# A transformer layer on one core: projection blocks spread over the steps, and the four score pairs of a step issued together ahead of the contexts

## The reference, cut to what matters

```python
def _L0_attn_ref(hidden_states, Wq, bq, Wk, bk, Wv, bv, Wo, bo):
    q = _split_heads(hidden_states @ Wq + bq)
    k = _split_heads(hidden_states @ Wk + bk)
    v = _split_heads(hidden_states @ Wv + bv)
    scores = jnp.einsum('bhqd,bhkd->bhqk', q, k) * scale
    probs = jax.nn.softmax(scores, axis=-1)
    ctx = jnp.einsum('bhqk,bhkd->bhqd', probs, v)
    return ctx.transpose(0, 2, 1, 3).reshape(b, s, h * d) @ Wo + bo

def _L0_ffn_ref(x, gate_w, up_w, down_w, gate_scale, up_scale, down_scale):
    gate = jax.nn.silu(_quantized_matmul(x, gate_w, gate_scale))
    up = _quantized_matmul(x, up_w, up_scale)
    return _quantized_matmul(gate * up, down_w, down_scale)

x = x + _layernorm(_L0_attn_ref(_layernorm(x), ...))
x = x + _layernorm(_L0_ffn_ref(_layernorm(x), ...))
```

## Time and profile before

| | |
|---|---|
| median of 3 runs | 1830.35 us (1827.28 to 1835.91) |
| the profiled execution's own time | 1833.34 us |
| its span, first to last instruction | 1831.5 us |
| instructions | 23069 |
| mean granted clock of TensorE | 0.941 |
| busy, share of the span | TensorE 89%, VectorE 71%, ScalarE 48%, GpSimd 27% |
| attention pass | until about 1190 us; the rest is the feed-forward pass |

### The profile page before, as it was taken

One profiled execution on the slowest core, in us unless ns is written; L12 is line 12 of the kernel. 1 busy time (PEld: TensorE's weight loads), 2 busy tenths in 40 slices (PEclk: granted clock), 3 DMA queues, 4 the chain that ended last, 5 costly groups with the idle time before them and its releaser, 6 DMA issues.

```text
span 1831.5 us, 23069 instructions
## 1 busy us (share of the span) xinstructions
PE 1621.8 (89%) x8328; PEld 755.8 (41%) x8328; DVE 1304.3 (71%) x2369; ACT 878.4 (48%) x1567; POOL 491.2 (27%) x384
## 2 busy tenths in 40 slices
PE   2599999999999999999999999835699999999996
PEld 1343343343343343343343343123355555555554
DVE  6279879879879879879879878779943543443344
ACT  2236756756756756756756756722222222222222
POOL 4012312212212212212212213345522222222222
PEclk9789999999999999999999999767899999999998
DMA  2402212212212212212112112233010210111020
GB/s 94 97 16 61 68 30 64 60 29 60 64 29 65 59 33 63 57 41 55 57 40 56 58 41 55 70 104 121 23 46 24 70 69 6 64 69 47 24 92 23
DMA packets 76441, 100.91 MB, mean 55 GB/s; under 512 B 15780, under 2 KB 40356, under 8 KB 76324
## 3 DMA queue, kind: packets, MB, share of 16 engines
q1 hardware_dynamic: 76328, 99.44, 18.4%
HBM read 51.65 MB, written 17.83 MB: 38 GB/s over the span
## 4 chain that ended last, share of the span: by engine, by line
PE 72%; DVE 22%; issue 3%; ACT 1%; POOL 1%; DMA 1%; SPq 0%; POOLq 0%; DVEq 0%; ACTq 0%
PE side L924 21%; PE ring L1322 17%; PE contexts L988 11%; PE down_sums L1337 9%; DVE maxima L778 9%; PE scores L976 8%; PE maxima_scores L961 5%; DVE y L737 2%; DVE w_magic L131 2%; DVE qkT L764 1%; DVE denominators L795 1%; DVE denominators L804 1%; DVE ctx_raw L800 1%; DVE xT_low L747 1%; ACT probs L692 1%
## 5 line engine op out<-in xcount | busy, mean ns | idle before, releaser
L778 DVE TENSOR_REDUCE maxima<-maxima_scores 128x1 f32<-128x512 f32 x1024 | 655.8, 678 | 123.7 <-PE maxima_scores L961 119.1
L692 ACT ACTIVATE probs<-scores 128x512 f32<-128x512 f32 x1024 | 554.2, 597 | 362.5 <-PE scores L976 359.5
L961 PE MATMUL maxima_scores<-k_stack,q_stack 64*128 64x512 f16 x1024 | 330.4, 394 | 34.8 <-DVE maxima L778 34.5
L976 PE MATMUL scores<-q_stack,k_stack 64*128 64x512 f16 x1024 | 329.1, 397 | 12.4 <-ACT probs L692 9.3
L988 PE MATMUL contexts<-probs,v_one 128*32 128x512 f32 x2048 | 288.6, 637 | 13.9 <-DVE ctx_raw L800 9.2
L1267 DVE SCALAR_TENSOR_TENSOR fuse<-ring,up_scale,gate 128x512 f32<-128x512 f32 x96 | 71.9, 749 | 263.2 <-PE ring L1322 261.8
L539 POOL TENSOR_TENSOR denominators<-denominators,reciprocals 128x512 f32<-128x512 f32 x33 | 42.4, 1284 | 707.1 <-ACT reciprocals L655 707.1
L1168 POOL TENSOR_TENSOR fuse_low<-fuse,fuse_high 128x512 fp32r<-128x512 f32 x96 | 123.1, 1282 | 368.4 <-ACT fuse_high L1202 368.4
L976 PEld LDWEIGHTS scores<-q_stack,k_stack 64*128 64x128 f16 x1024 | 64.6, 95 | 329.2 <-ACT probs L692 226.2
L1337 PE MATMUL down_sums<-down_q,fuse_high 128*128 128x512 f32 x384 | 171.4, 446 | 30.0 <-POOL fuse_low L1168 30.0
L1337 PE MATMUL down_sums<-down_q,fuse_low 128*128 128x512 f32 x384 | 155.7, 406 | 0.0
(11 more groups left out here) (151 smaller groups left out, 2418.9 us busy)
## 6 DMA issues: line engine op xcount, KB each, us to landing
q_stack<-qkT SPq DMA_DIRECT2D x192, 64.0 KB, 2.0
k_stack<-qkT SPq DMA_DIRECT2D x192, 64.0 KB, 2.0
x_rows<-in_L_attn_hidden_states SPq DMA_DIRECT2D x9, 1024.0 KB, 5.9
x_residual<-in_L_attn_hidden_states SPq DMA_DIRECT2D x36, 256.0 KB, 2.9
middle_rows<-y SPq DMA_DIRECT2D x36, 256.0 KB, 2.9
x_rows_ffn<-middle_rows SPq DMA_DIRECT2D x9, 1024.0 KB, 5.6
x_residual_ffn<-middle_rows SPq DMA_DIRECT2D x8, 1024.0 KB, 7.8
out_rows<-y_ffn SPq DMA_DIRECT2D x32, 256.0 KB, 2.2
```

Of the source, the lines that this page charges most:

```text
L692: act.activation(probs[:, n % 2, j, :], work[(GH * n + j) % RING][:], ACT.Exp, scale=float(D) ** -0.5).then_inc(p_full, 1)
L778: dve.tensor_reduce(maxima[:, g % 2, at:at + 1], bank[:], AX.X, ALU.max).then_inc(rot_free, 1)
L961: mm = pe.matmul(bank[:], q_st[half, s, qc * P:qc * P + P], k_st[half, s, :], start=True, stop=True)
L976: mm = pe.matmul(work[i % RING][:], k_st[half, s, c * P:c * P + P], q_st[half, s, :], start=True, stop=True)
```

## The change

Three things change, all in the attention pass.

1. `side_steps` is written anew. Before, 11 of the 32 steps hold a whole projection of 4 chunks, 10 hold 2 chunks, 4 hold the transposes of x, and 7 hold nothing. After it, 3 steps (0, 30, 31) hold 4 chunks, 26 hold 2, and 3 (21 to 23) hold none. The o projections stand in steps 5 to 8 and 13 to 16 instead of 5 to 8.
2. The transposes of x leave the `side` bank: they are items of the ring `maxima_scores` now, behind the four pairs of steps 13 to 16 (a fifth or sixth item). ScalarE makes their high part (`turned_high`) in the same step, behind the exponentials, and VectorE the low part as an item of its own behind the last reduction.
3. TensorE issues the four pairs of a step one behind the other, then the contexts of the step before, then the side chunks, then the items that are left.

With them move: the steps in which ScalarE inverts and refines (10/11, 20/21, 26/27 instead of 10/11, 18/19, 26/27), GpSimd's normalise (16, 21, 27 instead of 11, 19, 27), the statistics of the output rows (moments in step 18, normalisation in 19 and 20, residual sum on GpSimd in 22 and 25), and on the sync engine the `fill` (steps n % 4 == 0 instead of n % 4 == 1), residual loads (23 instead of 15), output rows (23 and 27 instead of 15 and 19) and the load of x (18 instead of 19). The counting of ring positions is replaced by one list for all turns, `rot_order` and `side_order`, without instructions of its own.

```diff
-    side_steps = {0: ("v", 3, 0, 2), 1: ("v", 3, 2, 4), 2: ("q", 2, 0, 2), 3: ("q", 2, 2, 4), 4: ("k", 2, 0, 4),
-                  5: ("o", 0, 0, 4), 6: ("o", 1, 0, 4), 7: ("o", 2, 0, 4), 8: ("o", 3, 0, 4),
-                  10: ("q", 3, 0, 2), 11: ("q", 3, 2, 4), 12: ("k", 3, 0, 4),
-                  14: ("x", 0, 0, 4), 15: ("x", 1, 0, 4), 16: ("x", 2, 0, 4), 17: ("x", 3, 0, 4),
-                  18: ("q", 0, 0, 2), 19: ("q", 0, 2, 4), 20: ("k", 0, 0, 4),
-                  26: ("q", 1, 0, 2), 27: ("q", 1, 2, 4), 28: ("k", 1, 0, 4),
-                  29: ("v", 0, 0, 4), 30: ("v", 1, 0, 4), 31: ("v", 2, 0, 4)}
+    side_steps = {0: ("v", 3, 0, 4), 1: ("q", 2, 0, 2), 2: ("q", 2, 2, 4), 3: ("k", 2, 0, 2), 4: ("k", 2, 2, 4),
+                  5: ("o", 0, 0, 2), 6: ("o", 0, 2, 4), 7: ("o", 1, 0, 2), 8: ("o", 1, 2, 4),
+                  9: ("q", 3, 0, 2), 10: ("q", 3, 2, 4), 11: ("k", 3, 0, 2), 12: ("k", 3, 2, 4),
+                  13: ("o", 2, 0, 2), 14: ("o", 2, 2, 4), 15: ("o", 3, 0, 2), 16: ("o", 3, 2, 4),
+                  17: ("q", 0, 0, 2), 18: ("q", 0, 2, 4), 19: ("k", 0, 0, 2), 20: ("k", 0, 2, 4),
+                  24: ("q", 1, 0, 2), 25: ("q", 1, 2, 4), 26: ("k", 1, 0, 2), 27: ("k", 1, 2, 4),
+                  28: ("v", 0, 0, 2), 29: ("v", 0, 2, 4), 30: ("v", 1, 0, 4), 31: ("v", 2, 0, 4)}
...
+    def rot_step(b, n):
...
+        out = [(maximum(i % MAXIMA), b + i // MAXIMA) for i in range(lo, lo + T) if b + i // MAXIMA < B]
         if lo % (GH * T) == 0:
...
+                out.append((("t", g), b + later))
+        if XT0 <= n < XT0 + T and b < B - 1:
+            out.append((("x", n - XT0), b + 1))
+        return out
...
@@ the sync engine, turn
+                if n % T == 0:
+                    later, g = divmod(n // T + SETS - 1, G)
+                    if b + later < B:
+                        if b * STEPS + n:
+                            sp.wait_ge(st_full, GH * (b * STEPS + n))
+                        fill(b + later, g)
...
@@ ScalarE
+        def turned_high(n, t):
+            p = rot_at[("x", t), n]
+            act.wait_ge(rot_full, p + 1)
+            act.copy(xT_h[:, :, t * P:t * P + P], rot[p % RING][:].rearrange("p (c t) -> p c t", c=KC)).then_inc(xTh, 1)
...
+                if n in (10, 20, 26):
+                    o = (10, 20, 26).index(n)
+                    invert(b * O + 1 + o, o)
+                if n in (11, 21, 28 if last else 27):
+                    o = n // 8 - 1
+                    refine(b * O + 1 + o, o)
...
+                if XT0 <= n < XT0 + T and not last:
+                    turned_high(b + 1, n - XT0)
...
@@ VectorE, reduce_maxima
+            elif item[0] == "x":
+                toks = slice(item[1] * P, item[1] * P + P)
+                dve.wait_ge(xTh, n * T + item[1] + 1)
+                dve.tensor_tensor(xT_l[:, :, toks], bank[:].rearrange("p (c t) -> p c t", c=KC),
+                                  xT_h[:, :, toks].bitcast(F32), ALU.subtract).then_inc(rot_free, 1)
...
@@ TensorE, turn
-                maxima_left = len(items) >= GH
-                for u in range(2):
-                    for j in range(2 * u, 2 * u + 2):
-                        score(b, n, j)
-                        if maxima_left:
-                            share(j)
-                    if u == 0 and n:
-                        contexts(b, n - 1)
+                beside = GH if len(items) >= GH else 0
+
+                for j in range(GH):
+                    score(b, n, j)
+                    if beside:
+                        rot_item(items[j][1], items[j][0])
+                if n:
+                    contexts(b, n - 1)
                 for c in range(lo, hi):
-                    side_piece(later * SIDE + side_at[what, i], later, (what, i), c)
-                share(GH if maxima_left else 0)
+                    side_piece(side_at[(what, i), later], later, (what, i), c)
+                for item, of in items[beside:]:
+                    rot_item(of, item)
```

More of the change, by code:

```diff
@@ L344, in attention_pass, with side_step @@
              ("v", 1), ("r", 8, 16), ("w", "o"), ("v", 2), ("r", 16, LEAD)])
-    start_at = {item: i for i, item in enumerate(item for item in start if item[0] not in "rw")}
-    assert all(start_at[item] == side_at[item] for item in ahead)
[L348 to L353, removed]
-    def side_step(n, last):
+    def side_step(b, n):
         what, i, lo, hi = side_steps.get(n, (None, 0, 0, 0))
-        return (None, 0, 0, 0) if last and of_next((what, i), n) else (what, i, lo, hi)
@@ L360, in side_end @@
-    def side_end(n, last):
+        later = b + of_next((what, i), n)
+        return (what, i, lo, hi, later) if later < B else (None, 0, 0, 0, 0)
+    def side_end(b, n):
         item = side_ends.get(n)
-        return None if last and item and of_next(item, n) else item
+        return (item, b + of_next(item, n)) if item and b + of_next(item, n) < B else None
     def of_next(item, n):
-        return 1 if item in ahead and n >= 14 else 0
-    fill_steps = {(4 * g - 11) % STEPS: g for g in range(G)}
+        return 1 if item in ahead and n >= NEXT else 0
@@ L844, in _ @@
             if item[0] == "r":
-                for i, p in start_rot(item[1], item[2]):
-                    reduce_maxima(0, i, p)
+                for part, n in rot_start(item[1], item[2]):
+                    reduce_maxima(n, part)
             elif item[0] == "w":
@@ L857, in turn @@
             for n in range(STEPS):
-                items = rot_step(n, last)
-                for k, (item, later, p) in enumerate(items):
-                    reduce_maxima(b + later, item, p)
-                    before = side_end(n - 1, last)
+                items = rot_step(b, n)
+                before = side_end(b, n - 1)
+                for k, (item, of) in enumerate(items):
+                    reduce_maxima(of, item)
                     if k == 0 and before:
-                        take(b + of_next(before, n - 1), before, b)
-                    if k == 1 and before and before[0] == "o":
-                        dve.wait_ge(side_free, b * SIDE + side_at[before] + 1)
-                        stats("out", y, before[1])
+                        take(before[1], before[0])
+                    if k == 1 and before and before[0][0] == "o":
+                        dve.wait_ge(side_free, side_at[before] + 1)
+                        stats("out", y, before[0][1])
                     if n in (1, 2) and k in (1, 2) and not last:
@@ L999, in _ @@
             if item[0] == "r":
[L1000 to L1002 removed]
+                for part, n in rot_start(item[1], item[2]):
+                    rot_item(n, part)
+            elif item[0] != "w":
                 if item[0] in "qkv":
```

205 lines of the change are left out of this document (99 added, 106 removed).

## The result

The changed kernel takes **1924.6 us** (median of 4 runs, 1921.4 to 1927.2) against 1831.5 us of the kernel before beside it (4 runs, 1827.3 to 1835.9): ratio 1.051, 95% interval 1.048 to 1.054. Forecast were 1947 us, within 1885 to 2015.

A forecast was written before the change was run, and what follows sets the result against it. TensorE was taken to bound the kernel, with 18.6 us of each 136.7 us turn waits and slow clock. Turns of 137.0 + 13 lags + 2.5 clock = 152.5, seven at +15.8 and the last +6.4, gave 1947 us, range 1885 to 2015.

The forecast's parts named there:

- the sum of a turn: One whole turn of the attention pass: 152.5 us against 136.7, +15.8 in each of seven turns.
- The block: Four pairs in a row on TensorE: at least 1.56 us instead of 1.08, +14.9 a turn over 31 steps.
- Lags: VectorE's and ScalarE's earlier work delays the next pairs: +13 us a turn, between 6 and 20.
- x items: Steps 13 to 16, behind the side chunks: the next step's fourth pair 1.0 us late, four times, +3.9 a turn.
- VectorE's leftovers: Steps 8, 9, 20 and 25 (takes, statistics, contexts, normalisation): 0.5 us each, +1.9 a turn.
- The transposed maxima: Two VectorE instructions between TensorE's transpose and the next first reduction: 0.5 us late, 6 x 0.53 = +3.2 a turn.
- The small transposes: 24 on TensorE in a turn, 16 of x and 8 of maxima: 3.5 us, an estimate, 6 at most.
- The clock: Two to three more slow-clock stretches in a turn beyond the waits, from more idle places: +2.5 us.
- The rival of the absorbed lags: VectorE's and ScalarE's extras vanish during contexts and side chunks; turn 137 to 138, kernel about 1840 us; chance 0.09.
- The rival that is faster: The fourth pair finds its banks free 0.7 us after the first; kernel about 1723 us; chance 0.05.
- The clock rival: TensorE's pauses in nearly every step lower its clock to a mean of 0.85; kernel about 2070 us; chance 0.10.
- the sync engine's queue: `fill` waits for a later k, `max_rows` behind it; waits possible in steps 24 and 26, about 1 us, not summed.

The follow-up runs named there:

- run 1: The changed kernel with the contexts back between the second and third pair, so the spread alone: 1806.5 us, ratio 0.987 against the kernel before.
- run 2: The kernel before with only the order changed, contexts behind the fourth pair: 1915.1 us, ratio 1.046.
- run 7: The changed kernel with ScalarE's exponential and VectorE's reduction reading 256 of the 512 columns: 1836.2 us, ratio 1.002 against the kernel before.
- run 3: The changed kernel with the transposes of x and of the maxima issued ahead of the side chunks: 1889.6 us, ratio 1.032 against the kernel before.
- run 5: The changed kernel with the edits of run 1 and run 3 together: 1803.1 us, ratio 0.985 against the kernel before.
- run 12: Run 10 with the residual and output rows moved behind the fill in the sync engine's queue: 1784.9 us, ratio 0.974 against the kernel before.
- run 8: Run 5 with VectorE's read of the contexts in every eighth step moved behind the fourth reduction: 1800.7 us, ratio 0.983 against the kernel before.
- run 10: Run 8 with ScalarE's `refine` and `invert` moved to later steps, with what depends on them: 1809.1 us, ratio 0.988 against the kernel before.
- run 11: Run 3 with the early contexts read and ScalarE's `refine` and `invert` later, four pairs still together: 1888.9 us, ratio 1.031 against the kernel before.

## Why the prediction was right, and where its sizes were off

**Right: what costs.** The even spread takes the old waits away, the four pairs in a row put a new one into every step, and nothing hides it. Runs 1 and 2 separate the two, run 7 shows that the answer of ScalarE and VectorE is what is waited for, and the waits view counts, in one turn, 22 waits of the scores for the exponential (10.1 us) and 8 of the maxima matmuls for VectorE (5.1), at the places named. The step with two chunks takes 4.11 ("at least 4.1"), TensorE is busy 86% ("about 85%").

**Off: the sum of a turn**, +12.4 instead of +15.8, in the turn from 704.91 to 854.03.
- The block: 1.52, not 1.56. 31 times 0.04, 1.2 less.
- Lags: 11.0, not 13 (10.7 in this turn as it ran, since TensorE at the lower clock in step 17 hides 0.3 of one). x items 4.1 (forecast 3.9); in steps 14 to 16 0.87 each, in 17 1.5. They hit the third pair first, not the fourth as forecast. ScalarE 3.4 (4.1). VectorE's leftovers 1.6 (1.9); step 20 has none. **The transposed maxima are the mis-sized term: 1.9, not 3.2**. The block is only 0.15 longer behind three of them, and 0.5 longer in steps 2, 10 and 18.
- The small transposes, an estimate in the prediction: they lengthen their steps by 2.7 together, not 3.5. The side chunks take 1.60 in a step and not 1.59, 0.3 more.
- The clock came out nearly as forecast, 2.8 for 2.5: 1.5 in the stretch around step 0 (10.28 - 8.74) and 1.2 in step 17 (5.93 - 4.71). Over six turns it is about 2.2, as not every turn has both.

With their signs (-1.2, -2.0, -0.8, +0.3, +0.3) these are the 3.4. The forecast for the profiled execution is 23 us too long (1950.3 against 1927.2): seven turns were put at 110.6 and cost 84.7, the last at 6.4 and cost 4.7, and 4.5 at the start and behind the attention were not forecast.

**The rival of the absorbed lags** was wrong for this kernel and right for its neighbour. With four pairs together the place of an item is worth 35 us (run 3), with the contexts between 3 (run 5). What failed is its premise that the time of the contexts and side chunks covers the extra work: that needs the extra work to come ahead of them.

**The rival that is faster** asked for an answer of 0.7 us. The shortened answer of run 7 brought the block to 1.25 and the kernel just level with before; at the real 1.13 it was out of reach.

**The clock rival** was wrong: 0.97 to 0.99 in the six turns, though TensorE now pauses in each step, and 0.95 to 0.99 in the same turns before. (Its reading of rows 1 was too kind: slices 2 and 3 of the kernel before, from 46 to 137 us, are at 7 and 8 tenths.) Two rules of the Trainium skill were weighed. That short pauses at each turn through the PSUM banks make the clock swing (TensorE: Matmul & The Clock Gate, A second HAM failure mode: psum-queue depth-cycling): the trace agrees only in a small part. The clock does fall, but in no more than three places of a turn, and the pause of 0.3 us in every plain step goes with 1.00. That a change of tiling mode drains TensorE (TensorEngine Tiling (Array Packing), Key Properties): by it alone the kernel would have taken 1780. A step has one change of tile kind less, yet side chunks still cost 1.60 and contexts 0.99, and the block 1.52; what the switch may save can't be seen behind the wait.

**Expected too much of the spread**: I had put at up to 18.6 us a turn what it could bring. Alone it brought 3.3 (136.7 to 133.4), and 25 us in all. The fixed sum was right for plain steps (3.66), but steps 8, 9, 14 to 17 and 26 kept waits for VectorE, ScalarE and DMAs. With the items first and the queues changed as well, run 12 has a turn of 129.6 (629.54 to 759.12).

**Costed at nothing**: the sync engine's queue. In the changed kernel ScalarE's take in step 26 meets the late fill in two turns only; in the turn from 1001.94 the block there is 3.43 instead of 2.73. In the shorter turns of runs 8 and 10 the wait is there in nearly all, and cost TensorE 0.8 us or more and 1.3 or more a turn. So nothing was nearly the right price for this kernel, whose turns take 149 us against 132 to 134 in those runs; with an even spread and shorter turns it is not.

## What to carry to other kernels

Where a ring of R banks feeds another engine, and its answer (here 1.13 us from a matmul to the next one into the same bank) takes longer than issuing R items (here 3 times 0.23), no more than R items should stand in a row on the producer, counted with every odd item that shares the ring. The work that needs no bank belongs between them, and items with a long answer go ahead of that work. An edit that brings much in one order may bring nothing in the other, so the cover decides and not the edit. Moving work later on one engine moves the DMAs that wait for it, and with them all that is queued behind in the issuing engine: look at the queue's order before the step's. Before a gain of some microseconds is put down to a schedule, compare the same stretch over all turns at the same granted clock.

## What was not expected of the hardware

The same stretch of the same kernel runs at either clock. From the contexts of step 31 to those of step 0, with the same matmuls (some records are missing) and VectorE and ScalarE busy as long, it takes 7.76 us at 1.00 or 9.3 at 0.82 in runs 1, 8, 10 and 12, and 8.74 at 1.00 or 10.3 at 0.83 in the kernel after. It is slow in four of seven places in the kernel after, in run 1 and in run 10, in three in run 8, in one in run 12 and in all seven in run 11. In the places looked at the low clock begins within 1.5 us of the end of a long wait of TensorE: of 1.42 us in step 0 of the kernel after and of run 12, of 2.85 us in the slowest step 26 of run 10. But the same wait of 1.42 us stands in the fast ones too. So neither the wait alone nor the schedule alone decides it; what does was not tried. One such stretch is worth 1.5 us, so differences of up to 10 us between two runs can be clock, and a part of run 12's gain over run 10 is.
